# A vision tower on one Trainium2 core: each image read once from the HBM, its two shifted copies made inside the SBUF

## The chip, the core and the metric

One core of one Trainium2 chip runs the whole program. The core has a matrix engine (PE), a vector engine (DVE), a scalar engine (ACT), a general engine (POOL), a sync engine (SP) that only issues transfers, and 16 DMA engines that carry them. The metric is device time of one execution in microseconds; lower is better.

## The reference

```python
# B, C, H, N_P, HID = 64, 3, 196, 14, 128;  P = 14;  SEQ = 197
patches = img.reshape(Bn, C, N_P, P, N_P, P).transpose(0, 2, 4, 1, 3, 5).reshape(Bn, N_P * N_P, IN_DIM)
tokens = einsum('bsd,hd->bsh', patches, W) + b            # IN_DIM = 3 * 14 * 14 = 588
h = concatenate([cls, tokens], axis=1) + pos
h = h + attn(layernorm(h))      # state = 0.9 * state + 0.1 * outer(k_t, v_t), read by q_t before the update
h = h + ffn(layernorm(h))       # routed grouped-query attention: 8, 4 or 1 key heads, one choice per image
```

All of it is float32. There are 64 images of 3 channels and 196 x 196 pixels, cut into 14 x 14 patches of 14 x 14 pixels.

## The kernel before

The program has four parts, one after the other: `prepare` (weights), `first` (patches, first attention, both layer norms), `route` (which of three weight sets each image takes) and `second` (the routed attention). The change is in `first` alone.

**Patches.** `first` holds the pixels of one image as an SBUF tile `img` of 126 partitions: 42 rows (`ROWS` = 3 channels x 14 pixel rows of a patch), three times over (`SHIFTS` = 3). A partition holds, for its channel and its pixel row within the patch, that row of each of the 14 patch rows, one after the other. The second set of 42 partitions holds the same pixels shifted left by 5 (`STEPS` = 5), the third by 10. One matmul then covers 126 of the 588 input numbers: for step s it reads every 14th pixel from s on, which is pixel s of each patch in the first set, s + 5 in the second, s + 10 in the third. Five matmuls (line 333; the profile records two instructions for each, so ten an image) make the 196 tokens of an image.

**Transfers.** There are four `img` tiles (`RING` = 4). SP runs over the images (lines 250 to 265). For image b it waits until the patches of image b - 4 are done (line 257) and issues nine transfers from the HBM (line 264): three shifts x three channels. Each goes to 14 partitions and brings 14 rows of 187 pixels (748 bytes; 186 pixels for the last shift) to each. All count up the semaphore `img_in` of their tile. All go through SP's one queue. A row of the tile has 192 places; the last ones are set to zero once (line 346).

**Order of work.** PE, DVE, ACT and POOL each run a software pipeline over images, one slot an image, in which stage k works on the image k slots back. PE's slot n does, in this order: transposes of image n - 6 (lines 277, 278), attention output of n - 5 (286 to 288), scores of n - 4 (295, 296), projections of n - 3 (303 to 309), transposes of n - 2 (317, 318) and n - 1 (324, 325), and last the patches of image n, for which it waits for `img_in` (line 329) and for DVE to have emptied the PSUM bank (`tokens_ready`, line 331). DVE adds the positions to the patches' result (line 420) at the end of its own slot.

In `second`, SP issues for each image eight copies within the SBUF that spread 128 partitions of `qk_hi` and `qk_lo` over 16 partitions each of `q_stack` and `k_stack` (line 602), one copy of 128 partitions by 792 bytes (`x_in`, line 583) and one of 128 partitions by 2048 bytes (`w_in`, line 586). This part is not changed.

Of the kernel before, what the change touches and what calls it, by code (L numbers as in the profile page):

```python
# [19 lines left out]
B, C, H, P, D = 64, 3, 196, 14, 128  # L20
N = H // P
# [6 lines left out]
ROWS = C * P  # L28
SHIFTS = 3
STEPS = (P + SHIFTS - 1) // SHIFTS  # L30
KROWS = SHIFTS * ROWS
WIDE = (N - 1) * P + STEPS
LR, DECAY, EPS = 0.1, 0.9, 1e-05
RING = 4
SPLIT = 4
# [32 lines left out]
def run_slots(engine, slot, lag):  # L68

    for n in range(2 * RING):  # L70
        slot(Image(n // RING, n % RING))
    with engine.Fori(2, B // RING) as turn:
        for u in range(RING):
            slot(Image(turn, u))
    for n in range(B, B + lag):
        slot(Image(n // RING, n % RING))
# [137 lines left out]
def first(nc, keep, image):  # L214

    with ExitStack() as ctx:
        sb = lambda name, shape, dt=F32: ctx.enter_context(nc.sbuf_tensor(name, shape, dt))
        sem = lambda name: ctx.enter_context(nc.semaphore(name))
        ident, add_t, x2t, h1, sums = (keep[k] for k in ("ident", "add_t", "x2t", "h1", "sums"))
        img = [sb(f"img{j}", [KROWS, N, WIDE + STEPS]) for j in range(RING)]  # L220
        h0t = sb("h0t", [D, SP])
        xhat1, xhat2 = sb("xhat1", [T, 2, D]), sb("xhat2", [T, 2, D])
        x1t = sb("x1t", [D, SP])
# [8 lines left out]
        TOK, ROW, XT1, QK, VV, SC, OUT, XT2 = range(8)  # L232
        set_up = sem("set_up")
        img_in = [sem(f"img_in{j}") for j in range(RING)]
        patches_done, tokens_ready, tokens_rowed = sem("patches_done"), sem("tokens_ready"), sem("tokens_rowed")
        stats1_done, mv1_done, var1_done, rstd1_done = (sem(x) for x in ("stats1_done", "mv1_done", "var1_done", "rstd1_done"))
        kept, norm1_done, turned1, x1t_ready = (sem(x) for x in ("kept", "norm1_done", "turned1", "x1t_ready"))
# [1 line left out]
        scores_done, att_ready, out_done, h1_ready = (sem(x) for x in ("scores_done", "att_ready", "out_done", "h1_ready"))  # L239
        stats2_done, mv2_done, var2_done, rstd2_done = (sem(x) for x in ("stats2_done", "mv2_done", "var2_done", "rstd2_done"))  # L240
        norm2_done, turned2, x2t_ready = (sem(x) for x in ("norm2_done", "turned2", "x2t_ready"))
        IMG_DMAS = 16 * SHIFTS * C
        LAG = 6
        block = ctx.enter_context(nc.Block())

# [3 lines left out]
        @block.sync  # L249
        def _(sp):  # L250
            sp.wait_ge(set_up, 1)

            def slot(b):
                if not b.exists():
                    return
                if b.has(RING):
                    sp.wait_ge(patches_done, b.i - RING + 1)
                for g in range(SHIFTS):
                    for c in range(C):
                        x0 = g * STEPS  # L260
                        cols = min(WIDE, H - x0)
                        src = image[bass.ds(b.i, 1), c, :, x0:x0 + cols].rearrange("a (i p) w -> (a p) i w", p=P)
                        r0 = g * ROWS + c * P
                        sp.dma_start(img[b.ring][r0:r0 + P, :, 0:cols], src).then_inc(img_in[b.ring], 16)
            run_slots(sp, slot, 0)

        @block.tensor
        def _(pe):
            pe.wait_ge(set_up, 1)

            def slot(n):
                b = n.back(6)
                if b.exists():
                    pe.wait_ge(norm2_done, b.i + 1)
                    if b.has(1):
                        pe.wait_ge(x2t_ready, b.i)
                    nc.tensor.transpose(ps[:, XT2, 0:T], xhat2[:, 0, :], ident[0:T, 0:T])
                    nc.tensor.transpose(ps[:, XT2, T:SP], xhat2[:, 1, :], ident[0:T, 0:T]).then_inc(turned2, 1)  # L278
                b = n.back(5)
                if b.exists():  # L280
                    pe.wait_ge(att_ready, b.i + 1)
                    pe.wait_ge(v_ready, b.i + 1)
                    if b.has(1):
                        pe.wait_ge(h1_ready, b.i)
                    v = v1[b.ring % 2]
                    nc.tensor.matmul(ps[0:T, OUT, 0:D], att[:, 0:T], v[:, 0, :], start=True, stop=True)
                    nc.tensor.matmul(ps[0:T, OUT, D:2 * D], att[:, T:SP], v[:, 0, :], start=True, stop=False)
                    nc.tensor.matmul(ps[0:T, OUT, D:2 * D], att[:, SP:SP + T], v[:, 1, :],
                                     start=False, stop=True).then_inc(out_done, 1)
                b = n.back(4)  # L290
                if b.exists():
                    pe.wait_ge(qk_ready, b.i + 1)
                    if b.has(1):
                        pe.wait_ge(att_ready, b.i)
                    nc.tensor.matmul(ps[0:T, SC, 0:SP], qkt[:, 1, 0:T], qkt[:, 0, :], start=True, stop=True)
                    nc.tensor.matmul(ps[0:T, SC, SP:SP + T], qkt[:, 1, T:SP], qkt[:, 0, T:SP],
                                     start=True, stop=True).then_inc(scores_done, 1)
                b = n.back(3)
                if b.exists():
                    pe.wait_ge(x1t_ready, b.i + 1)  # L300
                    if b.has(1):
                        pe.wait_ge(qk_ready, b.i)
                    nc.tensor.matmul(ps[:, QK, 0:SP], keep["wq"][:, :], x1t[:, :], start=True, stop=True)
                    nc.tensor.matmul(ps[:, QK, SP:2 * SP], keep["wk"][:, :], x1t[:, :],  # L304
                                     start=True, stop=True).then_inc(qk_done, 1)
                    if b.has(1):
                        pe.wait_ge(v_ready, b.i)
                    for t in range(2):
                        last = nc.tensor.matmul(ps[0:T, VV, t * D:(t + 1) * D], x1t[:, t * T:(t + 1) * T],
                                                keep["wvo"][:, :], start=True, stop=True)  # L310
                    last.then_inc(v_done, 1)
                b = n.back(2)
                if b.exists():
                    pe.wait_ge(norm1_done, b.i + 1)
                    if b.has(1):
                        pe.wait_ge(x1t_ready, b.i)
                    nc.tensor.transpose(ps[:, XT1, 0:T], xhat1[:, 0, :], ident[0:T, 0:T])
                    nc.tensor.transpose(ps[:, XT1, T:SP], xhat1[:, 1, :], ident[0:T, 0:T]).then_inc(turned1, 1)
                b = n.back(1)
                if b.exists():  # L320
                    pe.wait_ge(tokens_ready, b.i + 1)
                    if b.has(1):
                        pe.wait_ge(norm1_done, b.i)
                    nc.tensor.transpose(ps[0:T, ROW, 0:D], h0t[:, 0:T], ident[:, :])
                    nc.tensor.transpose(ps[0:T, ROW, D:2 * D], h0t[:, T:SP], ident[:, :]).then_inc(tokens_rowed, 1)
                b = n
                if b.exists():
                    pe.wait_ge(img_in[b.ring], IMG_DMAS * (b.round + 1))
                    if b.has(1):
                        pe.wait_ge(tokens_ready, b.i)  # L330
                    for s in range(STEPS):
                        cols = img[b.ring][:, :, s:s + (N - 1) * P + 1:P]
                        last = nc.tensor.matmul(ps[:, TOK, 0:S - 1].rearrange("p (i j) -> p i j", i=N),  # L333
                                                keep["w_tok"][0:KROWS, s, :], cols,
                                                start=(s == 0), stop=(s == STEPS - 1))
                    last.then_inc(patches_done, 1)
            run_slots(pe, slot, LAG)

        @block.vector
        def _(dve):  # L340
# [2 lines left out]
            nc.vector.memset(x1t[:, S:SP], 0.0)  # L343
            nc.vector.memset(x2t[:, :].rearrange("p (b s) -> p b s", b=B)[:, :, S:SP], 0.0)
            for j in range(RING):
                last = nc.vector.memset(img[j][:, :, H - (SHIFTS - 1) * STEPS:], 0.0)
            last.then_inc(set_up, 1)

            def slot(n):
# [551 lines left out]
```

## Time and profile before

| | us |
|---|---|
| median of 3 runs | 1726.66 |
| lowest, highest | 1703.04, 1736.02 |
| span of the profiled execution | 1706.0 |
| first patch matmul starts | 53.8 |
| last patch matmul starts | 548.1 |
| busy over the span: PE, DVE, ACT, POOL | 1135.4, 728.3, 442.3, 126.5 |

The span lies 20.7 us below the median and 3 us above the lowest run. The first stage takes about 29% of it; the rest, up to 1706, is nearly all the routed attention. The profile tells for each engine when it was busy, and when it stood idle what ended the wait. For the DMA engines it tells the busy share of the 16 and the gigabytes a second that they moved. A share near 1 says that there was always a packet under way; it can lie above 1, since packets of one engine overlap.

### The profile page before, as it was taken

To read this page: it belongs to the slowest core of one execution; us is meant where nothing else is said; L and a number is where in the kernel's file an instruction comes from. 1 tells how busy PE (TensorE), PEld (TensorE's weight loads), DVE (VectorE), ACT (ScalarE), POOL (GpSimd) and SP (SyncE) were. 2 spreads that over 40 slices of the span, in tenths; PEclk is the share of its full clock that TensorE was granted. 3 is DMA by queue.
4 is the path that set the end of the run, shared out by engine and by line. 5 is a ranking of instruction groups with operands and counts; after the bars stand their busy time and mean duration, and the time that the engine had idled before them with its cause. 6 is when DMAs were issued, how large, how long until landed. Compare 5 with 4: busy or idle time off the path is not lost.

```text
span 1706.0 us, 27035 instructions
## 1 busy us (share of the span) xinstructions
PE 1135.4 (67%) x7569; PEld 899.3 (53%) x7569; DVE 728.3 (43%) x2193; ACT 442.3 (26%) x1160; POOL 126.5 (7%) x142
## 2 busy tenths in 40 slices
PE   0377888999998337756565656565656565656566
PEld 0366666677666225545454545454545454545454
DVE  1145566666666533434343434343434343434343
ACT  0011111111112003323232323232323232323233
POOL 8011122112222000000000000000000000000000
PEclk9788999999999557878787878787878787878787
DMA  1999999999997034434343434343434343434342
GB/s 35 134 147 152 162 172 180 178 181 179 179 181 132 0 66 82 85 74 80 72 80 71 80 71 80 71 80 72 80 72 80 72 80 71 79 72 79 72 80 41
DMA packets 232436, 168.51 MB, mean 99 GB/s; under 512 B 21904, under 2 KB 224091, under 8 KB 232411
## 3 DMA queue, kind: packets, MB, share of 16 engines
q1 hardware_dynamic: 232410, 168.21, 57.6%
q8 instruction: 12, 0.20, 0.1%
q14 instruction: 14, 0.11, 0.0%
HBM read 85.69 MB, written 6.46 MB: 54 GB/s over the span
## 4 chain that ended last, share of the span: by engine, by line
PE 36%; DMA 9%; SPq 9%; DVE 7%; issue 5%; DVEq 0%; ACT 0%; ACTq 0%
PE ps L649 9%; DMA w_in<-sets 8%; PE ps L663 6%; PE ps L677 5%; PE ps L628 4%; PE ps L697 3%; SPq L579 3%; SPq L613 3%; DVE top L752 3%; PE ps L629 2%; PE ps L636 2%; SPq L583 2%; PE ps L709 2%; DVE h L781 2%; PE ps L687 1%
## 5 line engine op out<-in xcount | busy, mean ns | idle before, releaser
L752 DVE TENSOR_REDUCE top<-ps 99x2 f32<-99x394 f32 x512 | 282.0, 564 | 528.9 <-PE ps L649 523.2
L628 PE MATMUL ps<-x_in,w_in 128*128 128x198 f32 x128 | 65.3, 614 | 386.0 <-DMA w_in<-sets 359.9
L333 PE MATMUL ps<-img,w_tok 126*128 126x196 f32 x640 | 231.9, 522 | 87.8 <-DMA img<-in_x 87.8
L810 ACT ACTIVATE prob<-ps 99x396 f32<-99x396 f32 x512 | 228.3, 498 | 165.5 <-PE ps L663 165.3
L649 PE MATMUL ps<-k_stack,q_stack 96*99 96x198 f32 x1024 | 259.6, 361 | 1.7 <-DVE top L752 1.3
L628 PEld LDWEIGHTS ps<-x_in,w_in 128*128 128x128 f32 x128 | 32.0, 311 | 410.2 <-issue 399.6
L649 PEld LDWEIGHTS ps<-k_stack,q_stack 96*99 96x99 f32 x1024 | 193.7, 238 | 47.6 <-DVE top L752 30.8
L333 PEld LDWEIGHTS ps<-img,w_tok 126*128 126x128 f32 x640 | 133.3, 216 | 160.3 <-DMA img<-in_x 68.4
L663 PE MATMUL ps<-q_stack,k_stack 98*99 98x198 f32 x1024 | 183.3, 317 | 1.0 <-DMA q_stack<-top_rows 1.0
L663 PEld LDWEIGHTS ps<-q_stack,k_stack 98*99 98x99 f32 x1024 | 156.5, 226 | 2.2 <-DMA q_stack<-top_rows 1.4
L804 ACT ACTIVATE qk_hi<-ps 128x396 fp32r<-128x396 f32 x64 | 32.1, 501 | 444.0 <-PE ps L629 444.0
L677 PE MATMUL ps<-prob,v_ones 99*32 99x198 f32 (+1 forms) x2048 | 143.1, 352 | 0.0
L445 ACT ACTIVATE x2t<-ps 128x197 f32 (+1 forms) x64 | 21.5, 336 | 296.5 <-PE ps L278 296.5
L781 DVE TENSOR_TENSOR h<-ps,h 99x256 f32<-99x256 f32 x64 | 27.2, 424 | 144.1 <-PE ps L709 144.1
L430 POOL TENSOR_TENSOR rstd<-var,half 99x2 f32<-99x2 f32 x64 | 44.6, 697 | 358.2 <-DVE var L382 358.2
L420 DVE TENSOR_TENSOR h0t<-ps,add_t 128x196 f32<-128x196 f32 x64 | 23.3, 364 | 104.5 <-PE ps L333 104.4
L697 PE MATMUL ps<-ident,mix 128*99 128x128 f32 x256 | 66.2, 412 | 0.6 <-ACT mix L817 0.6
L452 ACT ACTIVATE qkt<-ps,bq 128x198 f32<-128x198 f32 x64 | 27.3, 427 | 124.7 <-PE ps L304 124.7
L677 PEld LDWEIGHTS ps<-prob,v_ones 99*32 99x32 f32 (+1 forms) x2048 | 41.4, 111 | 33.7 <-issue 6.3
L412 DVE TENSOR_SCALAR xhat<-ps,mv,rstd 99x128 f32<-99x128 f32 x128 | 46.6, 406 | 23.2 <-POOL rstd L434 23.2
L697 PEld LDWEIGHTS ps<-ident,mix 128*99 128x99 f32 x256 | 55.0, 283 | 1.3 <-ACT mix L817 1.3
L629 PE MATMUL ps<-x_in,w_in 128*128 128x198 f32 x128 | 55.5, 537 | 0.0
(140 smaller groups left out, 1519.5 us busy)
## 6 DMA issues: line engine op xcount, KB each, us to landing
img<-in_x SPq DMA_DIRECT2D x384, 143.2 KB
img<-in_x SPq DMA_DIRECT2D x192, 142.4 KB
w_in<-sets SPq DMA_DIRECT2D x64, 256.0 KB, 2.3
q_stack<-qk_hi SPq DMA_DIRECT2D x128, 99.0 KB, 3.2
k_stack<-qk_hi SPq DMA_DIRECT2D x128, 99.0 KB, 3.8
q_stack<-qk_lo SPq DMA_DIRECT2D x128, 99.0 KB, 4.3
k_stack<-qk_lo SPq DMA_DIRECT2D x128, 99.0 KB, 4.8
x_in<-x2t SPq DMA_DIRECT2D x64, 99.0 KB, 2.0
```

The lines of the kernel that those rows point to most:

```text
L333: last = nc.tensor.matmul(ps[:, TOK, 0:S - 1].rearrange("p (i j) -> p i j", i=N), keep["w_tok"][0:KROWS, s, :], cols, start=(s == 0), stop ...
L579: choice = sp.value_load(keep["choice"][0:1, bass.ds(b.i, 1)], min_val=0, max_val=len(KV) - 1)
L613: sp.dma_start(out[bass.ds(b.i, 1), t * T:t * T + keys(t), :].rearrange("a s e -> (a s) e"), h2[b.ring % 2][0:keys(t), t, :]).then_inc(sto ...
L628: nc.tensor.matmul(ps[:, QK, 0:SP], w_in[b.ring][:, 0, :], x_in[b.ring][:, :], start=True, stop=True)
L629: nc.tensor.matmul(ps[:, QK, SP:2 * SP], w_in[b.ring][:, 1, :], x_in[b.ring][:, :], start=True, stop=True).then_inc(qk_done, 1)
L649: last = nc.tensor.matmul(ps[0:T, M0 + c % 2, j * SP:(j + 1) * SP], q_stack[b.ring][0:BIAS_ROW, h, qt * T:(qt + 1) * T], k_stack[b.ring][0 ...
L663: last = nc.tensor.matmul(ps[0:T, E0 + c % 2, j * SP:(j + 1) * SP], k_stack[b.ring][:, h, kt * T:(kt + 1) * T], q_stack[b.ring][:, h, :], ...
L677: last = nc.tensor.matmul(ps[32 * j:32 * j + 32, MIX, g * SP:(g + 1) * SP], v_ones[b.ring % 2][0:keys(kt), kt, 4 * g + j, :], prob[0:keys( ...
L697: last = nc.tensor.transpose(ps[0:T, FIN, at:at + D], mix[:, g, t * T:(t + 1) * T], ident[:, :])
L752: nc.vector.tensor_reduce(top[:, c // 4, 2 * (c % 4):2 * (c % 4) + 2], cols, AX.X, ALU.max, negate=True).then_inc(m_read, 1)
L781: nc.vector.tensor_tensor(h2[b.ring % 2][:, :, :], two(ps[0:T, FIN, 0:2 * D]), two(h1[:, bass.ds(b.i * 2 * D, 2 * D)]), ALU.add).then_inc( ...
L810: nc.scalar.activation(prob[:, c % 4, :], ps[0:T, E0 + c % 2, 0:CHUNK], ACT.Exp, scale=DK ** -0.5).then_inc(exp_done, 1)
```

## The change

`img` becomes 126 partitions by 14 x 196 pixels, without gaps. SP issues three transfers an image from the HBM (one a channel, 14 partitions, 14 rows of 784 bytes each) into the first 42 partitions. One slot later it waits for these to have landed and issues two transfers within the SBUF. Each copies the 42 partitions, from pixel 5 or 10 on, to the next or the last 42 partitions, as one run of 2739 or 2734 pixels (10956 or 10936 bytes) a partition. PE waits for a further semaphore, `img_shifted`. The zeros at the end of a row become fewer.

```diff
-        img = [sb(f"img{j}", [KROWS, N, WIDE + STEPS]) for j in range(RING)]
+        img = [sb(f"img{j}", [KROWS, N * H]) for j in range(RING)]
...
+        img_shifted = [sem(f"img_shifted{j}") for j in range(RING)]
...
-        IMG_DMAS = 16 * SHIFTS * C
+        IMG_DMAS, SHIFT_DMAS = 16 * C, 16 * (SHIFTS - 1)
...
-                for g in range(SHIFTS):
+            def slot(n):
+                b = n
+                if b.exists():
+                    if b.has(RING):
+                        sp.wait_ge(patches_done, b.i - RING + 1)
                     for c in range(C):
-                        x0 = g * STEPS
-                        cols = min(WIDE, H - x0)
-                        src = image[bass.ds(b.i, 1), c, :, x0:x0 + cols].rearrange("a (i p) w -> (a p) i w", p=P)
-                        r0 = g * ROWS + c * P
-                        sp.dma_start(img[b.ring][r0:r0 + P, :, 0:cols], src).then_inc(img_in[b.ring], 16)
-            run_slots(sp, slot, 0)
+                        src = image[bass.ds(b.i, 1), c, :, :].rearrange("a (i p) w -> (a p) i w", p=P)
+                        sp.dma_start(img[b.ring][c * P:(c + 1) * P, :].rearrange("p (i w) -> p i w", w=H),
+                                     src).then_inc(img_in[b.ring], 16)
+                b = n.back(1)
+                if b.exists():
+                    sp.wait_ge(img_in[b.ring], IMG_DMAS * (b.round + 1))
+                    for g in range(1, SHIFTS):
+                        width = N * H - g * STEPS
+                        sp.dma_start(img[b.ring][g * ROWS:(g + 1) * ROWS, 0:width],
+                                     img[b.ring][0:ROWS, g * STEPS:N * H]).then_inc(img_shifted[b.ring], 16)
+            run_slots(sp, slot, 1)
...
                     pe.wait_ge(img_in[b.ring], IMG_DMAS * (b.round + 1))
+                    pe.wait_ge(img_shifted[b.ring], SHIFT_DMAS * (b.round + 1))
...
-                        cols = img[b.ring][:, :, s:s + (N - 1) * P + 1:P]
+                        cols = img[b.ring][:, :].rearrange("p (i w) -> p i w", w=H)[:, :, s:s + (N - 1) * P + 1:P]
...
-                last = nc.vector.memset(img[j][:, :, H - (SHIFTS - 1) * STEPS:], 0.0)
+                last = nc.vector.memset(img[j][:, N * H - (SHIFTS - 1) * STEPS:], 0.0)
```

## Rows read from the trace of the kernel before

**Rows 1.** The page, part 2: the span in 40 slices of 42.65 us.

```profile
PE   0377888999998337756565656565656565656566
...
PEclk9788999999999557878787878787878787878787
DMA  1999999999997034434343434343434343434342
GB/s 35 134 147 152 162 172 180 178 181 179 179 181 132 0 66 82 85 74 80 72 80 71 80 71 80 71 80 72 80 72 80 72 80 71 79 72 79 72 80 41
```

**Rows 2.** Stretches of the first stage: length, busy us by engine, clock, DMA share, GB/s.

```profile
53.70:63.60 9.90, 4.19 (x13) 3.26 (x13) 2.33 (x9) 0.00 (x0) 0.73 (x1) 0.84 1.02 133
...
100.00:150.00 50.00, 38.91 (x186) 31.08 (x187) 27.02 (x109) 7.13 (x27) 8.58 (x12) 0.90 1.01 153
...
400.00:450.00 50.00, 45.09 (x236) 34.93 (x234) 32.51 (x129) 9.77 (x35) 9.43 (x14) 0.97 1.00 180
```

**Rows 3.** Line 333, the patch matmuls: ns each, first and last start, waits, followers.

```profile
L333 PE MATMUL ps<-img,w_tok x640: 498/516/696, 53.8 to 548.1; 126*128 126x196 f32 x160
...
  DMA img<-in_x: 156.2, 102
...
  DVE h0t L420: 104.4, 59
```

**Rows 4.** Waits within 400 to 500 us: waiting engine, releaser, us, times, longest.

```profile
PE ps L333 <- DMA img<-in_x: 9.1, 11, 0.9
...
DVE h0t L420 <- PE ps L333: 12.1, 12, 1.1
...
DVE h L354 <- PE ps L288: 9.9, 14, 1.4
```

**Rows 5.** Timeline, two slots from 420.79 on, and the last image: start, length, engine.

```profile
420.79 3.62 PE L333 MATMUL ps<-img,w_tok 126*128 126x196 f32 x10 [0.74 <-DMA img<-in_x]
...
424.23 0.27 PE L277 MATMUL ps<-ident,xhat 99*128 99x99 f32 x1
...
427.00 0.27 PE L325 MATMUL ps<-ident,h0t 128*99 128x128 f32 x1
...
428.14 3.62 PE L333 MATMUL ps<-img,w_tok 126*128 126x196 f32 x10 [0.86 <-DMA img<-in_x]
...
431.80 0.36 DVE L420 TENSOR_TENSOR h0t<-ps,add_t 128x196 f32<-128x196 f32 x1 [1.03 <-PE ps L333]
...
434.36 0.27 PE L325 MATMUL ps<-ident,h0t 128*99 128x128 f32 x1
...
545.02 3.62 PE L333 MATMUL ps<-img,w_tok 126*128 126x196 f32 x10 [0.47 <-DMA img<-in_x]
```

**Rows 6.** The page, part 6: issues on SP's queue, KB each, us to landing.

```profile
img<-in_x SPq DMA_DIRECT2D x384, 143.2 KB
img<-in_x SPq DMA_DIRECT2D x192, 142.4 KB
w_in<-sets SPq DMA_DIRECT2D x64, 256.0 KB, 2.3
q_stack<-qk_hi SPq DMA_DIRECT2D x128, 99.0 KB, 3.2
...
k_stack<-qk_lo SPq DMA_DIRECT2D x128, 99.0 KB, 4.8
x_in<-x2t SPq DMA_DIRECT2D x64, 99.0 KB, 2.0
```

**Rows 7.** Issues of image transfers on SP (line 264): ns each, first and last start.

```profile
L264 SPq DMA_DIRECT2D img<-in_x x576: 320/678/1235, 41.1 to 536.9; - x192
```

**Rows 8.** Stretches with SBUF copies: w_in (385 and 396 GB/s), then the eight stack copies.

```profile
1002.70:1003.20 0.50, 0.00 (x0) 0.00 (x0) 0.00 (x0) 0.00 (x0) 0.00 (x0) 0.50 1.01 385
...
1002.80:1003.10 0.30, 0.00 (x0) 0.00 (x0) 0.00 (x0) 0.00 (x0) 0.00 (x0) 0.50 1.04 396
...
1011.00:1012.00 1.00, 1.00 (x15) 0.71 (x8) 0.73 (x2) 0.59 (x3) 0.00 (x0) 1.00 1.20 103
...
1010.00:1013.00 3.00, 2.47 (x26) 1.86 (x26) 2.15 (x6) 1.96 (x5) 0.00 (x0) 1.00 1.12 110
```

**Rows 9.** Timeline of the start of the stage: first issues, first two images.

```profile
41.15 9.56 SPq L264 DMA_DIRECT2D img<-in_x  x16
...
53.78 3.70 PE L333 MATMUL ps<-img,w_tok 126*128 126x196 f32 x10 [14.10 <-DMA img<-in_x]
...
63.57 3.73 PE L333 MATMUL ps<-img,w_tok 126*128 126x196 f32 x10 [5.18 <-DMA img<-in_x]
```

**Rows 10.** The page, parts 2 and 3: all bytes moved, and HBM traffic.

```profile
DMA packets 232436, 168.51 MB, mean 99 GB/s; under 512 B 21904, under 2 KB 224091, under 8 KB 232411
...
HBM read 85.69 MB, written 6.46 MB: 54 GB/s over the span
```

More of the change, by code:

```diff
@@ L31 @@
 KROWS = SHIFTS * ROWS
-WIDE = (N - 1) * P + STEPS
 LR, DECAY, EPS = 0.1, 0.9, 1e-05
@@ L251, in _ @@
             sp.wait_ge(set_up, 1)
[L253 to L257, printed above, removed]
-                for g in range(SHIFTS):
-                    for c in range(C):
-                        x0 = g * STEPS
-                        cols = min(WIDE, H - x0)
-                        src = image[bass.ds(b.i, 1), c, :, x0:x0 + cols].rearrange("a (i p) w -> (a p) i w", p=P)
-                        r0 = g * ROWS + c * P
-                        sp.dma_start(img[b.ring][r0:r0 + P, :, 0:cols], src).then_inc(img_in[b.ring], 16)
-            run_slots(sp, slot, 0)
+            def slot(n):
[3 more added lines that the diff above has]
+                        sp.wait_ge(patches_done, b.i - RING + 1)
+                    for c in range(C):
+                        src = image[bass.ds(b.i, 1), c, :, :].rearrange("a (i p) w -> (a p) i w", p=P)
[9 more added lines that the diff above has]
+            run_slots(sp, slot, 1)
         @block.tensor
```

## The prediction

> **What bounds the kernel now.** I read the slices of the span first [rows 1]. Between slices 2 and 12 the DMA share is 9 in every slice, and it is 0 in slice 14. In the rest of the span it is 3 or 4. So only the stage that reads images has its DMA engines always at work, and that is the stage that the change touches. Next come the stretches of that stage [rows 2]. The share is 1.00 to 1.02 throughout, but the rate is not constant: 133 GB/s at the first images, 153 later, 180 from the middle on. So a busy share of 1 doesn't fix a rate; what an engine moves in a packet's time has changed, with the same transfers.
>
> Who waits for whom says what ends last. The patch matmuls wait for image data [rows 3]. In 100 us of steady state PE loses 9.1 us to it, in 11 of some 14 slots, and DVE's waits are for PE's own results [rows 4]. The timeline shows one slot [rows 5]: patches at 420.79, the next at 428.14, so 7.35 us an image. PE has finished line 325 at 427.27 and stands idle 0.86 us until the image is there. DVE's line 420 comes 1.03 us after it was ready for it, so it isn't late either. Without the wait an image would take PE about 7.35 - 0.85 = 6.5 us. That is the next bound below: PE itself.
>
> An image is 6 x 143.2 + 3 x 142.4 = 1286 KB [rows 6], which is 1.317 MB. At 180 GB/s this takes 7.3 us: the period is the DMA's. The first patches start at 53.78, the last image's at 545.02 [rows 9, 5], so 63 periods take 491.2 us, 7.80 each on average. Of that, 63 x 7.35 = 463 is the steady rate and some 28 us are the slow beginning (9.8 us between the first two images [rows 9]).
>
> **What the change does, part by part.**
>
> *Transfers from the HBM.* Nine become three, of 14 partitions each as before, with rows of 784 instead of 748 bytes: 42 x 2744 x 4 = 0.461 MB an image. At the steady 180 GB/s that is 2.56 us; at the 133 of the first images it would be 3.5. I take 2.56: these are the same kind of transfer, one third of them.
>
> *Copies in the SBUF.* Two of 42 partitions by 10.95 KB: 0.460 + 0.459 = 0.919 MB an image. The trace of before has no copy of this shape, so I bound it. Below: `w_in` goes from 128 to 128 partitions in rows of 2048 bytes at 385 to 396 GB/s [rows 8]; at that the copies take 2.4 us. Above: the eight stack copies of `second`, 128 partitions into 16 at a time, run at 103 to 110 GB/s once they pile up, at a share of 1.12 to 1.20 [rows 8]; at 103 the copies take 8.9 us. Rows there are 792 bytes; but `x_in` has such rows too, 128 partitions to 128, and lands in 2.0 us where a stack copy of the same 99 KB needs 3.2 to 4.8 [rows 6]. So it is less the length of the rows than the few partitions that holds them back. Long rows alone won't save the copies, then. What counts is how many different partitions are under way at one time. Both copies have 42, all read from the same first 42. That is nearest to the image loads, whose DMAs have 14 partitions each and several in flight, and which run at 133 GB/s when they begin together and at 180 when the engines have drifted apart [rows 2]. I take 180: 0.919 MB / 180 GB/s = 5.1 us.
>
> The Trainium skill ("SBUF — State Buffer", the section on the DMA port swizzle) says that groups of four partitions share a port, that partitions p and p + 32 share the same one, and that 0 to 63 reach only 8 of 16 ports, at about 27.2 GB/s each. The stack copies agree: 16 partitions are four ports by it, 109 GB/s, and the row has 103 to 110 [rows 8]. By that rule partitions 0 to 3 and 32 to 35 are on one port, so both copies read 16 rows of 10.95 KB through it, 6.4 us an image at least, against my 5.1; whether reads are held to it as writes are, no row here shows.
>
> *The sum.* 2.56 + 5.1 = 7.67 us an image on the DMA engines, against 7.35 now. The total of bytes rises by 4.8% (the gaps of the tile are now filled), and by my choice of rates nothing else changes. This is still above PE's 6.5. I don't count the slow beginning again: long copies between the loads let engines drift apart sooner. 63 x 7.67 = 483, against 491.2: -8 us.
>
> *SP's queue.* Nine issues of 678 ns median [rows 7] are 6.1 us of every 7.35; five make 3.4 us. Nothing waited for issues, so this gives nothing. The new wait on `img_in` stands in front of the two copies, and behind it in SP's order stands only the next image's load. At slot n it asks for a load that was issued one slot, about 7 us, earlier; copies of this size land in 2 to 5 us [rows 6]. The load of image n is issued before it, so loads don't wait for copies. Then the copy of n - 1 has until PE gets there: at patches_done(n - 4) PE still has n - 3 and n - 2 ahead, over 14 us, against some 2.6 for the load in front, 5.1 and some 2 to landing. So latency is covered, with 4 us to spare; with copies at 103 GB/s (8.9) it would just not be.
>
> *Start.* Before, the first patches begin 12.6 us after the first issue, at 53.78 [rows 9]. After: three issues (2 us), load and landing (4 to 5), copies behind the second load (2.6 + 5.1 + 2). That is 14 to 16 us, so +2, less 0.3 for the smaller memset. It is within the rounding of the sum.
>
> *PE.* Same matmuls and the same step of 14 pixels, so 3.62 us an image [rows 5]. [...] `route` and `second` are unchanged; 0.
>
> On the profile's own time: 1706.0 - 8 = 1698. The median of the runs is 20.7 above the span, and I carry the difference over: 1726.66 - 8 = 1719.
>
> **The rivals.**
>
> *A. PE becomes the bound.* Reads of the SBUF aren't held back by few partitions, only writes are, and the copies write to 84 partitions, twice as many different ones as the loads. Then they run at, say, 300 GB/s, 3.1 us; with the load 5.6, below 6.5. For it: `w_in` at 385 to 396 GB/s with long rows [rows 8]. Against: 14 engines on 42 source partitions. It decides from 6.5 - 2.56 = 3.9 us, that is 233 GB/s. Time: 63 x 6.5 = 410, -82; the clock at the beginning (0.84 to 0.90 against 0.97 [rows 2]) and the added wait give 5 back: -77, 1650.
>
> *B. My forecast:* copies at the loads' rate, 1719. Its own range: DMA period 7.1 (copies at 200 GB/s) to 8.3 (160), -44 to +32: 1683 to 1759.
>
> *C. The narrow source decides.* All DMA engines read both copies out of the same 42 partitions, and since both copies are issued together and the engines take their rows in the same order, they meet at the same partitions, as the loads did at the first images (133 GB/s) or the stack copies (103). At 133 the copies take 6.9 us, with the load 9.5: 63 x 9.5 = 599, +107, 1834. At 103 it would be 8.9 + 2.56 = 11.5, +233. It makes the kernel over 2% slower from 8.35 us an image on, copies below 159 GB/s. For it: rates of 103 to 133 are seen in this very trace. Against: the loads did drift to 180, and the copies' rows are ten times longer, so engines fall out of step sooner. The skill's port rule belongs here: 6.4 us on the worst port plus the load, if they don't overlap, is 9.0. If they do overlap, it is 6.5 to 7 and ends as B or A.
>
> *D. Latency.* The chain load, wait, copy, wait gets longer than the ring of four covers. By the sum above it has 4 us to spare, so it counts only together with C.
>
> **How the numbers follow.** A 0.31, B 0.44, C 0.25 (with D). 2% of 1726.66 is 34.5 us, about what a measurement of this kernel can tell from no change; it is 0.55 us an image: faster below 7.25, slower above 8.35. A lies whole in faster. Of B, 0.08 is below 7.25, the rest is within 2%. Of C, 0.03 is under 8.35. Faster 0.39, same 0.39, slower 0.22. The range takes A in with 10 us below it (1640), and of C what lies up to 8.9 us an image (1795); about 0.1 is left out above and 0.07 below and beyond.
>
> **What would show it.** The period between patches in steady state: 7.6 to 7.8 (B), 6.5 with no DMA wait (A), over 8.3 (C). GB/s in the middle of the stage near 180 at a share of 1 (B), near 210 at a share under 1 (A: 1.38 MB in 6.5 us), 145 to 165 at a share of 1 (C). Bytes read from HBM fall from 85.7 MB [rows 10] by the 84.3 of the images and come back by 64 x 0.461 = 29.5, to about 31; total DMA bytes rise from 168.5 [rows 10] by 64 x 0.063 = 4 MB, to 172.5. The landing time of the copies: about 8 us (B), under 6 (A), over 10 (C). SP's queue must show waits for `img_in` or `patches_done` now. Spans of `second` must agree to within a few us; if they don't, the difference isn't the change's. I would be most wrong if the long rows were slower by themselves than rows of 784 bytes, which no row excludes, or if the copies were spread over fewer engines than the loads.

## The result and the profile after

The changed kernel takes 1.0164 times the time of the kernel before (95% interval 1.0131 to 1.0198), 1.6% more: inside the 2% that I called "same", but with the whole interval on the other side of the forecast of -0.5%. The ratio compares fast runs alone and leaves out those more than 1.5% above the fastest, which are many of the kernel before, as it scatters widely (1683.50 to 1808.13; the changed one 1718.98 to 1745.78). Over all 20 runs of each the medians are 1723.51 and 1721.16, 0.1% apart. So what the rest explains, the profiled spans of 1722.5 and 1706.0 (+16.5 us), is the changed kernel against one of the better executions of the kernel before.

The last image's patches now start at 561.16 instead of 545.02, +16.1 us. What follows takes 1161.4 us after and 1161.0 before. So the whole difference lies in the first stage. It is made of the first patches' start (57.95 instead of 53.78, +4.2) and the 63 periods (7.99 instead of 7.80 us each, +12.0).

The page of the changed kernel, parts 2 and 3 (compare [rows 1, 10]):

```profile
PEclk9989999999999756787878787878787878787877
DMA  1998998999898034443434343434444444444342
GB/s 37 141 164 183 169 179 167 173 180 181 172 175 167 0 55 79 77 80 72 79 71 79 73 78 76 75 75 74 78 73 79 75 78 74 76 74 78 72 79 40
DMA packets 158962, 172.54 MB, mean 100 GB/s; under 512 B 18319, under 2 KB 145242, under 8 KB 153562
...
HBM read 30.90 MB, written 6.46 MB: 22 GB/s over the span
```

The change did what it says: 30.9 MB read from the HBM instead of 85.7, and 172.5 MB moved in all, as forecast. The rates are near those of before: 167 to 183 GB/s from the fourth slice to the twelfth, where before had 152 to 181. Next the stretches that answer to [rows 2] (length, busy us of PE, PEld, DVE, ACT, POOL, clock, DMA share, GB/s):

```profile
53.70:63.60 9.90, 4.43 (x12) 3.38 (x12) 1.05 (x4) 0.00 (x0) 0.00 (x0) 1.00 0.86 142
...
100.00:150.00 50.00, 41.79 (x216) 33.84 (x216) 29.59 (x117) 8.37 (x30) 8.56 (x12) 0.92 0.91 176
400.00:450.00 50.00, 43.95 (x223) 34.54 (x223) 30.13 (x118) 8.79 (x32) 8.65 (x13) 0.93 0.88 175
```

The beginning is a little faster than before (176 against 153 GB/s from 100 to 150 us), the steady part a little slower (175 against 180), at a DMA share of 0.88 to 0.92 instead of 1. Before, the period fell from 9.8 to 7.37 us (images 20 to 50) and stayed; now it is 10.3 at first and 7.87 in the same images, and it wanders between 7.1 and 9.3. The line of the patches and SP's issues, against [rows 3, 7] (ns min/median/max, first and last start):

```profile
L338 PE MATMUL ps<-img,w_tok x640: 497/514/666, 58.0 to 564.2; 126*128 126x196 f32 x160
L260 SPq DMA_DIRECT2D img<-in_x x192: 320/2179/3469, 40.8 to 543.4; - x192
...
L267 SPq DMA_DIRECT2D img<-img x128: 747/774/1794, 48.3 to 550.6; - x128
```

A load takes SP 2179 ns to issue, where it took 678. SP's timeline shows two slots (start, length):

```profile
420.15 5.78 SPq L260 DMA_DIRECT2D img<-in_x  x3
426.05 1.59 SPq L267 DMA_DIRECT2D img<-img  x2
427.92 6.09 SPq L260 DMA_DIRECT2D img<-in_x  x3
434.15 1.58 SPq L267 DMA_DIRECT2D img<-img  x2
```

SP is at work all the time, most of it inside the three loads. So it was before, with nine shorter issues an image:

```profile
419.66 16.76 SPq L264 DMA_DIRECT2D img<-in_x  x21
```

This does not leave the DMA engines without work. In both kernels each image transfer posts 14 small packets (4 bytes, for the semaphore) when it lands, so 14 engines carry it. By the starts and lengths of the packet records, 14 or more packets are under way during 95% of the time from 200 to 400 us in the changed kernel, and what is missing to 14 in the rest adds up to 1.3% of the 14. So the share of 0.92 where before had 1.00 is mostly less overlap between packets, and not idle engines. The matrix engine stands idle before its patches in the same stretch:

```profile
420.90 3.58 PE L338 MATMUL ps<-img,w_tok 126*128 126x196 f32 x10 [1.28 <-issue]
...
427.07 0.27 PE L329 MATMUL ps<-ident,h0t 128*99 128x128 f32 x1
428.72 3.58 PE L338 MATMUL ps<-img,w_tok 126*128 126x196 f32 x10 [1.38 <-issue]
```

So the stage is bound by the transfers as before; in these slots the matrix engine waits 1.3 us an image for them instead of 0.85 [rows 5]. "Issue" here is the wait for `img_shifted`, whose end the trace doesn't tie to a transfer each time.

### The profile page after: what moved, and what is told of

It is laid out like the page before. It is cut to its first block, busy times and chain, and to the rows that moved or that the text cites. A ratio compares the mean times of both kernels' runs of the same rounds, so it can differ in the third digit from the quotient of the medians.

```text
span 1722.5 us, 26149 instructions
## 1 busy us (share of the span) xinstructions
PE 1142.6 (66%) x7569; PEld 906.4 (53%) x7569; DVE 729.1 (42%) x2193; ACT 442.4 (26%) x1160; POOL 126.2 (7%) x142
## 4 chain that ended last, share of the span: by engine, by line
PE 36%; DMA 9%; SPq 9%; DVE 7%; issue 5%; DVEq 0%; ACT 0%; ACTq 0%
PE ps L654 9%; DMA w_in<-sets 8%; PE ps L668 6%; PE ps L682 5%; PE ps L633 4%; PE ps L702 3%; SPq L584 3%; SPq L618 3%; PE ps L634 2%; DVE top L757 2%; PE ps L641 2%; SPq L588 2%; PE ps L714 2%; DVE h L786 2%; PE ps L692 1%
## 5 line engine op out<-in xcount | busy, mean ns | idle before, releaser
L786 DVE TENSOR_TENSOR h<-ps,h 99x256 f32<-99x256 f32 x64 | 27.2, 425 | 145.5 <-PE ps L714 145.5
```

What stands on the lines that cost most here:

```text
L786: nc.vector.tensor_tensor(h2[b.ring % 2][:, :, :], two(ps[0:T, FIN, 0:2 * D]), two(h1[:, bass.ds(b.i * 2 * D, 2 * D)]), ALU.add).then_inc( ...
```

## The experiments

All are measured against the kernel before. "Period" is from one image's patches to the next; "steady" is its mean over images 20 to 50. Where a kernel ran once, only its profile is used. Packet times are means over 200 to 400 us unless said otherwise.

### What loads and copies cost

**Loads alone.** The copies, their wait and PE's wait for them are taken out. The whole tile is set to zero at the start, here and in the other runs that leave copies out.

```diff
-                b = n.back(1)
-                if b.exists():
-                    sp.wait_ge(img_in[b.ring], IMG_DMAS * (b.round + 1))
-                    for g in range(1, SHIFTS):
-                        ... (both copies)
-            run_slots(sp, slot, 1)
+            run_slots(sp, slot, 0)
...
-                    pe.wait_ge(img_shifted[b.ring], SHIFT_DMAS * (b.round + 1))
```

> Left out: both copies, so the second and third set of 42 partitions stay zero and the tokens lack two thirds of their sums. The three loads an image stay. Three theories of the 7.8 us an image of the changed kernel. Narrow source: both copies read the same 42 partitions, and DMA engines that meet there get less each. Bytes: an engine's time goes by bytes (about 180 GB/s in all) wherever they come from. Queue: all transfers go through SP's one queue, and engines that are done stand idle while SP is held up. All three expect loads alone to take about 2.6 us an image, so the matrix engine bounds at 6.5 us, 63 periods are 410 us and the kernel is 90 us shorter than the changed one. If the period stays over 7, the loads cost more than a third of what they did.

Span 1610.5, steady period 6.23 at a clock of 1.00. Stretches of it:

```profile
55.00:70.00 15.00, 9.81 (x30) 7.86 (x31) 3.94 (x16) 0.34 (x1) 0.73 (x1) 1.00 1.00 97
...
300.00:400.00 100.00, 100.00 (x547) 78.20 (x546) 76.31 (x306) 22.32 (x80) 22.91 (x32) 1.00 0.52 74
```

The matrix engine bounds, as every theory said; its floor is 6.23, not the 6.5 that I read from a clock of 0.97. But the first row is the find: while SP issues as fast as it can, these loads keep the DMA engines at a share of 1.00 and move only 97 GB/s. At that rate an image's 0.461 MB takes 4.75 us, not 2.56.

**One copy.** `for g in range(1, SHIFTS)` becomes `for g in range(1, 2)`.

> Left out: the second copy, so the last 42 partitions stay zero. Narrow source and bytes: 2.6 (loads) + 2.6 (one copy) = 5.2 us of DMA an image, under the 6.5 of the matrix engine, so a period of 6.5 and a span some 90 us below the changed kernel's. Queue: SP's issues shrink only by 0.8 us an image, period near 7.0.

Span 1622.5, steady period 6.26, later 6.2 to 6.5 and partly bound by transfers:

```profile
300.00:400.00 100.00, 99.87 (x534) 77.05 (x533) 75.09 (x301) 21.87 (x80) 22.85 (x32) 1.00 0.95 144
```

Of the 12 us over the run with loads alone, 5.8 are a later first image. The period I had expected (6.5, or 5.2 of DMA work) hid how near to full the DMA engines are already.

**Three copies.** A third copy goes to a spare tile; SP waits two slots later for it to have landed.

```diff
+                    at = (1 + b.ring % 2) * ROWS
+                    if b.has(2):
+                        e = b.back(2)
+                        sp.wait_ge(img_extra[e.ring], 16 * (e.round + 1))
+                    sp.dma_start(extra[at:at + ROWS, 0:N * H - STEPS],
+                                 img[b.ring][0:ROWS, STEPS:N * H]).then_inc(img_extra[b.ring], 16)
```

> Added: a third copy an image, of the first 42 partitions into a spare tile that nothing reads. It gives the price of one copy where the DMA engines bound. Bytes: 7.8 + 2.6 = 10.4 us an image, span +160 us against the changed kernel. Narrow source: at least 10.4, rather 11, since one more reader meets in the same partitions. Queue: only the 0.8 us of one more issue, 8.6 us, +50 us.

Span 1921.1, period 11.19: +3.2 us for a copy of 0.460 MB, 144 GB/s. This is dearer than the 2.55 of my sum and rules out that only the 0.8 us of an issue counts. The rows of the copies take 893 ns, against 816 with two copies, so a third copy also makes the others dearer. The narrow source had forecast 11; but any cause by which packets under way hold each other up would do the same, and the next run speaks against a shared source.

### Where the copies read, how long their rows are, whose queue they use

**The second copy from the first one's partitions**, one slot later.

```diff
+                    sp.dma_start(img[b.ring][ROWS:2 * ROWS, 0:N * H - STEPS],
+                                 img[b.ring][0:ROWS, STEPS:N * H]).then_inc(img_once[b.ring], 16)
+                b = n.back(2)
+                if b.exists():
+                    sp.wait_ge(img_once[b.ring], 16 * (b.round + 1))
+                    sp.dma_start(img[b.ring][2 * ROWS:3 * ROWS, 0:N * H - 2 * STEPS],
+                                 img[b.ring][ROWS:2 * ROWS, STEPS:N * H - STEPS]).then_inc(img_shifted[b.ring], 16)
```

> Changed: the second copy is taken from the first copy's 42 partitions (shifted by 5 once more) and issued one slot later, so the two copies of a slot read different partitions. Same bytes, same number of transfers. Narrow source: the period falls clearly below 7.8, to 6.5 to 7.2, the span by 40 to 80 us against the changed kernel; the packets of the copies get shorter. Bytes and queue: nothing changes, 7.8 us, span within 5 us. The ring of four may be too short for the longer chain; then the waits for the copy are long though the DMA share is far below 0.9.

1733.50 us median, span 1735.4, steady period 8.17: slower, not faster. The waits of SP and a stretch:

```profile
SPq L261 <- PE ps L342: 288.0, 60, 6.0
...
300.00:400.00 100.00, 82.40 (x415) 65.80 (x414) 57.91 (x229) 17.03 (x62) 17.17 (x24) 0.92 0.92 167
```

SP waited 288 us for patches to be done, since the longer chain uses up the ring of four, and a load takes it 321 ns to issue now. But the last sentence of the expectation asked for a share far below 0.9 as the sign of a ring that is too short, and the share is 0.92; 14 or more packets are under way during 96% of the time from 200 to 400 us. So the DMA engines bound here too. The other sign of the narrow source was shorter packets of the copies: they take 831 ns, against 816 in the changed kernel. So that both copies read the same 42 partitions is not what makes them dear, as far as packets show it. The run leaves open what an engine meets within one copy, whose partitions lie side by side as before.

**Short rows** in the copies: 14 rows of 764 or 744 bytes a partition instead of one of 10.95 KB.

```diff
-                        sp.dma_start(img[b.ring][g * ROWS:(g + 1) * ROWS, 0:width],
-                                     img[b.ring][0:ROWS, g * STEPS:N * H]).then_inc(img_shifted[b.ring], 16)
+                        sp.dma_start(wide(img[b.ring][g * ROWS:(g + 1) * ROWS, :])[:, :, 0:cols],
+                                     wide(img[b.ring][0:ROWS, :])[:, :, g * STEPS:H]).then_inc(img_shifted[b.ring], 16)
```

> The changed kernel, with its copies cut into 14 rows a partition of 764 and 744 bytes instead of one run of 10.95 KB; same partitions, 3% fewer bytes. If long rows are what helps the copies, the copies get dearer: span +60 us or more. If only the partitions that are under way count, the period stays 7.6 to 8.0, or falls a little since engines drift apart sooner; span within 25 us.

Span 1769.5.

```profile
300.00:400.00 100.00, 81.78 (x402) 65.53 (x401) 56.78 (x227) 16.57 (x60) 17.15 (x24) 0.90 0.96 161
```

Of the +47 us over the changed kernel, 11.8 are the start (the whole tile is set to zero first), and 63 x (8.58 - 7.99) = 37 are the period. Between the two expectations: short rows cost the copies some 0.6 us an image, though with 3% fewer bytes. Long rows help, by less than a tenth of the period.

**Copies on the scalar engine's queue**, two images ahead; SP only loads.

```diff
+            def shift(b):
...
+                act.wait_ge(img_in[b.ring], IMG_DMAS * (b.round + 1))
+                for g in range(1, SHIFTS):
+                    width = N * H - g * STEPS
+                    act.dma_start(img[b.ring][g * ROWS:(g + 1) * ROWS, 0:width],
+                                  img[b.ring][0:ROWS, g * STEPS:N * H]).then_inc(img_shifted[b.ring], 16)
...
                     nc.scalar.activation(x1t[:, 0:S], ps[:, XT1, 0:S], ACT.Copy).then_inc(x1t_ready, 1)
+                shift(n.back(-AHEAD))
```

> The changed kernel with the two copies issued from the scalar engine's queue, two images ahead, instead of SP's. Same transfers. Queue (SP held up in front of full rings, engines idle at a DMA share of 0.9): the period falls from 7.9 towards 7.0, span -50 us. Neighbouring partitions: loads and copies meet in the same partitions as before; period 7.5 to 8.1, span within 25 us of the changed kernel. In between would say that both count.

> The changed kernel with the copies issued from the scalar engine's queue once more, now timed, since one look gave 1698 us with a period of 7.16 us in the middle of the stage. If a second queue lets the DMA engines work on loads and copies side by side, the ratio to before is 0.98 to 1.00, 1 to 3% under the changed kernel. If that look was chance, it is 1.01 to 1.02 like the changed kernel's.

The first run took 1698.05 us, with a steady period of 7.16:

```profile
300.00:400.00 100.00, 91.50 (x478) 70.43 (x477) 67.15 (x266) 19.70 (x72) 20.00 (x28) 0.98 0.92 194
```

Run ten times more, the kernel is at 0.991 of before (0.983 to 0.999), where the changed kernel had 1.016. Its runs spread from 1686.45 to 1736.42, and the medians give 0.992, where the changed kernel's give 1.001; so the gain is 1 to 2.5%. In the second profile the period jumps between 6.2 and 11.6, with a steady mean of 8.09. The gain doesn't come from idle engines put to work, as the queue theory had it: in the first profile the share is the 0.92 of the changed kernel, and it is the packets that are shorter, 69 ns for a load's row and 763 for a copy's, against 76 and 816. In the second they are as long as the changed kernel's (76 and 830), and so is the time, 1721.32 us. Why they differ is not shown. A second queue doesn't bring the period near 6.23, and it makes it erratic.

### Rows of the tile in another order

A transfer of 14 partitions is carried by 14 DMA engines, as the 14 small packets at its landing say. I take it that each engine has one partition, which no view shows. In these kernels the 14 partitions no longer lie side by side; the columns of the weights are ordered to match, so that the result is the same sum.

**The kernel before, its loads to every ninth partition.**

```diff
-                        r0 = g * ROWS + c * P
-                        sp.dma_start(img[b.ring][r0:r0 + P, :, 0:cols], src).then_inc(img_in[b.ring], 16)
+                        r0 = g * C + c
+                        sp.dma_start(img[b.ring][r0:KROWS:SHIFTS * C, :, 0:cols], src).then_inc(img_in[b.ring], 16)
```

> The kernel before, with its nine loads an image, but the rows of the tile in another order: a transfer goes to every ninth partition (0, 9, 18, ...) instead of 14 in a row; the weights are ordered to match. Same bytes, packets, issues. Loads alone into 42 partitions ran at 98 GB/s, the nine into 126 at 133 to 180. If that is because DMA engines that write to neighbouring partitions at the same time hold each other up, then transfers whose 14 partitions lie apart must run freely from the first image on: period at the matrix engine's floor of 6.23 us, 63 x (7.80 - 6.23) = 99 us less than before, span near 1610, packets near 40 ns instead of 62. If it is bytes, the HBM or SP's queue, the period stays 7.3 to 7.8 and the span within 10 us of before.

1794.43 us, 1.044 of before (1.035 to 1.053): both theories missed. The stretch and SP's issues say what happened:

```profile
300.00:400.00 100.00, 74.19 (x356) 61.42 (x357) 50.35 (x200) 13.99 (x51) 15.44 (x22) 0.86 0.54 141
...
L265 SPq DMA_DIRECT2D img<-in_x x576: 809/822/1103, 41.1 to 627.0; - x192
```

The share fell from 1.00 to 0.54, so the transfers did get cheap: the packet records have a median of 36 ns for a row of 748 bytes, where before it was 62 (300 to 500 us). But a load with a step between its partitions takes SP 822 ns to issue, min 809, whereas the same load to neighbours takes 320 when nothing holds it up (321 median in the run with loads alone). With some 0.2 us between issues, nine are 9.2 us an image, and that is the mean period of the stage (9.19). SP's issuing had become the bound.

**The changed kernel in that order**, six copies of 14 partitions instead of two of 42.

```diff
-                        sp.dma_start(img[b.ring][c * P:(c + 1) * P, :].rearrange("p (i w) -> p i w", w=H),
+                        sp.dma_start(img[b.ring][c:KROWS:SHIFTS * C, :].rearrange("p (i w) -> p i w", w=H),
...
-                        sp.dma_start(img[b.ring][g * ROWS:(g + 1) * ROWS, 0:width],
-                                     img[b.ring][0:ROWS, g * STEPS:N * H]).then_inc(img_shifted[b.ring], 16)
+                        for c in range(C):
+                            sp.dma_start(img[b.ring][g * C + c:KROWS:SHIFTS * C, 0:width],
+                                         img[b.ring][c:KROWS:SHIFTS * C, g * STEPS:N * H]).then_inc(img_shifted[b.ring], 16)
```

> The changed kernel with the same order of rows: three loads and, since a transfer can only step evenly, six copies of 14 partitions an image instead of two of 42. Same bytes. Neighbouring partitions: loads 42 x 40 ns = 1.7 us, copies 6 x 0.46 us = 2.7 us on each engine, so 4.4 us, and the matrix engine bounds at 6.23: span near 1610, ratio to before 0.94. Bytes or queue: 7.8 us or, with four more issues of 0.8 us, up to 9, span 1720 to 1800.

1725.04 us, mean period 8.13. Again the packets are short (419 ns for a row of 10.95 KB, where the changed kernel has 816 on average, and the share is 0.49), and again SP is the bound:

```profile
300.00:400.00 100.00, 84.84 (x425) 67.69 (x424) 58.82 (x233) 17.42 (x63) 17.17 (x24) 0.91 0.49 170
...
303.18 2.94 SPq L261 DMA_DIRECT2D img<-in_x  x3
306.26 4.79 SPq L269 DMA_DIRECT2D img<-img  x6
311.33 2.94 SPq L261 DMA_DIRECT2D img<-in_x  x3
```

2.94 + 4.79 and the gaps are 8.15 us. The expectation had priced four more issues at 0.8 us only for the other theory; this one needed them as well.

**Woven.** Both findings together: neighbours apart, and only five issues.

```diff
-                        sp.dma_start(img[b.ring][c * P:(c + 1) * P, :].rearrange("p (i w) -> p i w", w=H),
+                        sp.dma_start(img[b.ring][c * SHIFTS:KROWS:SHIFTS * C, :].rearrange("p (i w) -> p i w", w=H),
...
-                        sp.dma_start(img[b.ring][g * ROWS:(g + 1) * ROWS, 0:width],
-                                     img[b.ring][0:ROWS, g * STEPS:N * H]).then_inc(img_shifted[b.ring], 16)
+                        sp.dma_start(img[b.ring][g:KROWS:SHIFTS, 0:width],
+                                     img[b.ring][0:KROWS:SHIFTS, g * STEPS:N * H]).then_inc(img_shifted[b.ring], 16)
...
+                        src = w_rows[:, :].rearrange("h (c p j) -> h p c j", p=P, j=P)[:, :, :, g * STEPS + s]
+                        to = w_perm[:, s, 0:KROWS].rearrange("h (p c g) -> h p c g", c=C, g=SHIFTS)
+                        last = nc.vector.tensor_copy(to[:, :, :, g], src)
```

> The changed kernel with its rows woven: pixel row p, channel c, shift g lies in partition 9p + 3c + g, the weights ordered to match. So a load goes to every ninth partition and a copy from every third partition to its neighbour, and there are three loads and two copies as in the changed kernel. Packets should be as short as in the run with six copies (near 48 and 419 ns). SP's own time a slot: 3 x 0.98 + 2 x 0.80 = 4.5 us, so neither the DMA engines (42 x 48 ns + 6 x 0.42 us = 4.5 us each) nor SP reach the matrix engine's 6.23 us. Neighbouring partitions and SP's issue time together: period 6.23 and span near 1615, ratio to before 0.94. If something else holds these transfers at 176 GB/s, the period stays 7.8 and the span near 1720.

1607.38 us, 0.939 of before (0.927 to 0.950), with runs from 1604.06 to 1609.04. Period 6.23. This is 5 to 7% under the kernel before; the fastest of that kernel's 13 runs beside it took 1703.58, and the fastest of the changed kernel's 20 took 1718.98. Its stretches, line and SP's waits:

```profile
60.00:100.00 40.00, 38.59 (x186) 30.30 (x186) 24.07 (x91) 6.45 (x22) 6.50 (x10) 1.00 0.91 247
...
300.00:400.00 100.00, 100.00 (x550) 78.38 (x549) 76.29 (x307) 22.47 (x81) 22.86 (x32) 1.00 0.75 221
...
L261 SPq DMA_DIRECT2D img<-in_x x192: 810/861/1566, 40.8 to 424.9; - x192
...
L268 SPq DMA_DIRECT2D img<-img x128: 753/793/1349, 46.1 to 428.8; - x128
...
SPq L261 <- PE ps L339: 68.0, 57, 1.4
```

The matrix engine is busy 100.00 of 100 us. The same bytes in the same number of transfers as in the changed kernel go at 221 GB/s, and at 247 before the ring is full, and now SP waits for PE. The rows of the copies take 554 ns, not the 419 that I had expected from the run with six copies; there was room for it.

### Which neighbours

**Loads alone, far apart from each other, neighbours within each.** Channel c goes to partitions 42c to 42c + 13 (`img[b.ring][c * ROWS:c * ROWS + P, :]`).

> Left out: both copies, as in the run with loads alone; the three loads go to partitions 0 to 13, 42 to 55 and 84 to 97 instead of 0 to 41. Each transfer still fills 14 neighbours. If what counts is that the DMA engines write to neighbours within one transfer, the loads run at the same 98 GB/s in the first images and the DMA share at 6.23 us an image stays 0.52. If what counts is that all transfers in flight share few partitions, engines that have drifted to another transfer no longer meet: 130 to 180 GB/s before the ring is full, share 0.35 to 0.45.

**Loads alone, woven** (`img[b.ring][c * SHIFTS:KROWS:SHIFTS * C, :]`).

> Left out: both copies; the three loads go to every ninth partition, as in the woven kernel. It gives the price of the loads by themselves when no two DMA engines write to neighbours: the share at 6.23 us an image should be 42 x 14 x 47 ns / (16 x 6.23 us) = 0.28 or less, against 0.52 with neighbours. The span is the matrix engine's in both, 1600 to 1612.

The first of the next rows is of the run with loads far apart:

```profile
55.00:70.00 15.00, 10.14 (x32) 7.06 (x33) 3.94 (x16) 0.34 (x1) 1.27 (x2) 1.00 1.00 102
...
300.00:400.00 100.00, 100.00 (x549) 78.39 (x548) 76.15 (x305) 22.49 (x81) 22.85 (x32) 1.00 0.54 74
```

and these are of the woven loads:

```profile
55.00:70.00 15.00, 12.03 (x37) 9.46 (x38) 4.67 (x18) 0.34 (x1) 1.43 (x2) 1.00 0.66 174
...
300.00:400.00 100.00, 100.00 (x549) 78.39 (x548) 76.30 (x305) 22.34 (x80) 22.90 (x32) 1.00 0.29 74
```

To spread the three transfers over the whole tile changes nothing (102 against 97 GB/s, share 0.54 against 0.52). To pull apart the 14 partitions of each takes the share from 0.52 to 0.29 at the same 74 GB/s, and the rate while SP issues freely from 97 to 174 GB/s at a share of only 0.66. The HBM is read in the same way in all three runs, so the difference is on the side of the SBUF. What counts is which partitions lie side by side within a transfer; that its 14 engines work on them at the same time is the likely reason.

The Trainium skill ("SBUF — State Buffer", section "Door 1: The DMA port swizzle") has four neighbouring partitions on one port, at about 27.2 GB/s a port. By that page 0, 9, 18 to 117 are 14 different ports, and 14 neighbours only four; four ports make 109 GB/s, and the rows show 97 to 102. The trace agrees with it for these writes. The page gives bandwidth by how many of the ports a transfer's partitions reach; the far-apart run agrees that for transfers issued one after another it isn't their sum that counts. It isn't the whole account: the kernel before, with nine transfers of 14 neighbours each, runs at 133 GB/s at its first images and at 180 later [rows 2], above the 109 of four ports.

## Why the prediction was wrong

**The price of the loads: the step that failed.** I wrote "these are the same kind of transfer, one third of them" and took 180 GB/s, so 2.56 us. That was the rate of nine transfers an image, some 25 images into the stage; that their engines had drifted apart by then is my explanation, and no row shows it. Loads by themselves run at 97 GB/s, 4.75 us (loads alone, 55 to 70 us). In the changed kernel, beside copies, their packets average 76 ns: 42 of them are 3.2 us on each engine. Packets of one engine overlap, so this can't be set against 2.56 as it stands: by the same count the kernel before has 67 ns, 126 packets and 8.4 us in a period of 7.37. In like terms the loads come to some 2.8 us, an estimate from 76 and 67 ns and rows 5% longer. The clue stood in [rows 2]: 133 GB/s at the first images, which I used as an upper end (3.5 us) and then left.

**The price of the copies: about right, for a reason only half right.** I took 5.1 us. Six rows of 816 ns on each engine make 4.9. That few partitions hold copies back, not short rows, was argued from [rows 6, 8] and is borne out in part: the same copies with neighbours apart take 419 ns a row (six copies), half, and short rows alone cost 0.6 us an image. But it isn't their number alone: in both orders 42 partitions are read and 84 written.

**The sum.** 7.67 was forecast, 7.87 measured in the steady part. In rates, the mix ran at 175 GB/s where I took 180 for loads and copies alike. Of the 0.2 us, some 0.1 is the 1.3% in which fewer than 14 packets were under way.

**The slow beginning: the second step that failed.** In the steady part my own 7.67 was slower than the 7.35 of before, by 20 us over 63 periods. It became a gain of 8 only because I set it against the average of before, 7.80, and left out a slow beginning of 28 us, with the sentence "long copies between the loads let engines drift apart sooner". The beginning did become shorter (7.1 to 7.5 us already from image 8 to 11, where before had 8.2 to 9.0), but the period went up again and never settled. 63 x 7.67 = 483 was forecast, 503.2 measured: 12.9 us of the difference are the steady period, 7.1 the beginning. With that, -8 becomes +12.0.

**Start.** +2 forecast, +4.2 measured (57.95). My terms were not added up rightly: 2 + 4.5 + 2.6 + 5.1 + 2 is 16.2 us after the first issue, not "14 to 16", and against 12.6 that is +3.6. The last three terms held: the copies of the first image, issued at 48.35, need 9.6 us where I had 9.7.

**SP's queue: right in its price, wrong in its picture.** I counted issues (3.4 us an image) and said that they give nothing. SP is in fact at work all the time, held up inside the loads, and waits for `img_in` only 8 times, 18.3 us in all. But so it was in the kernel before, and the DMA engines have work meanwhile: at most the 1.3% above, 0.1 us an image, is idle time that could be laid to SP. A second queue made the kernel 1 to 2.5% faster, but where its profile shows a gain, the packets are shorter, which is another thing. I had also taken an issue's duration for its cost: the 678 ns of [rows 7] is a load held up; free, it is 320. Where the transfers got cheap, in the two spread kernels, SP's issues did become the bound.

**The rivals.** A didn't come: PE is the bound only in the woven kernel and where copies are left out. Its floor was 6.23 instead of 6.5, with a clock of 1.00 when PE never waits. The price of one more semaphore wait, which I put into the 5 us that A gives back, no run shows: the woven kernel has that wait and loads alone don't, and both have a period of 6.23. C, the narrow source, named the mechanism, DMA engines meeting at the same partitions, but laid it on the two copies' common source and priced it at +107. The chain of copies shows no gain from parting the sources, the loads' writing is held up as well, and in the mix it came to +12. D, latency, was no cost in the steady part; the chain of two copies used the ring up and started 5.6 us later, yet its DMA engines stayed at work.

**What stays open.** Whether the copies are held at the partitions that they read or those that they write: the order of the tile changes both at once. Why nine transfers an image of 14 neighbours each begin at 133 GB/s and rise to 180, while three of them run at 97 to 102. Why the changed kernel's period wanders (7.1 to 9.3), and why copies on a second queue have shorter packets.

## What to carry to other kernels

Price a transfer by how many of its partitions lie side by side, not by its bytes alone; a rate measured in a mix of transfers doesn't hold for a third of the mix. If the rows of a tile may stand in any order (a contraction over partitions doesn't care), choose the order in which the partitions of one transfer lie apart, and then look at the issuing engine again, since a step between partitions makes issues dearer. A DMA share of 1 at less than the rate seen elsewhere in the trace is not yet a limit: here, at a share of 0.9 to 1, the same load and copy bytes went at 175 GB/s in one order of partitions and at 247 in another. And a share below 1 need not be idle engines; count the packets under way before blaming the engine that issues.

## What the runs showed of the hardware that I had not expected

- Three loads of 14 neighbours each: 97 GB/s at a share of 1.00; the same loads to every ninth partition: 174 GB/s at 0.66. Packets of 748 bytes have a median of 62 ns with neighbours and 36 apart; rows of 10.95 KB take 816 and 419 (six copies) or 554 (woven).
- A load from the HBM takes SP 320 ns to issue to neighbouring partitions and 810 to 860 to partitions with a step; a copy within the SBUF takes 750 to 790 with or without one.
- With copies queued in front of it, a load holds SP for 2.2 us (median), and everything behind it on SP with it.
- With neighbours the kernel before scatters from 1683.50 to 1808.13 (20 runs); with its loads to every ninth partition, bound by SP, it takes 1793.82 to 1795.28, and the woven kernel 1604.06 to 1609.04 (4 runs each). That neighbours cause the scatter was not tested.
